# Memory of the first two cross batches split in the dense phase, their keys and values projected ahead of the turn of the queries

## What is computed

```python
attn_out = jnp.where(vm, ctx @ v_dense, ctx @ l_dense)
hidden_states = residual + attn_out
ci = rms_norm(hidden_states, ln_post_cross_w)
cq = heads(ci @ cq_w, NH, CHD)                 # cross queries, 16 heads of 16
ckv = encoder_outputs @ ckv_w                  # encoder_outputs is the memory
ck, cv = jnp.split(ckv, 2, axis=-1)
cctx = sdpa(heads(cq), heads(ck), heads(cv), causal=False)
hidden_states = hidden_states + cctx @ cdense_w
```

## Time and profile before

| | us |
|---|---|
| median of three runs | 2365.92 |
| the profiled execution: span from its first to its last instruction | 2358.2 |
| median less span | 7.7 |
| TensorE busy | 2198.0 (93%) |
| VectorE busy | 1336.0 (57%) |
| ScalarE busy | 1072.2 (45%) |
| GpSimd busy | 880.1 (37%) |
| mean granted TensorE clock | 0.984 of full speed |

### The profile page before, as it was taken

How to read it: one execution, slowest core, us unless ns; L and a number is a source line. 1 busy time by engine, 2 the same in 40 slices (tenths; PEclk the granted TensorE clock), 3 DMA queues, 4 the chain that set the end, 5 groups by cost and what they waited for, 6 DMA issues and landing times.

```text
span 2358.2 us, 46947 instructions
## 1 busy us (share of the span) xinstructions
PE 2198.0 (93%) x19542; PEld 1834.5 (78%) x19542; DVE 1336.0 (57%) x1919; ACT 1072.2 (45%) x1842; POOL 880.1 (37%) x738
## 2 busy tenths in 40 slices
PE   6899998999989989987999999998899999999998
PEld 5799986887766668876777777776788888888887
DVE  5655545877779994436666666663534444435332
ACT  4344434343167774533555555553543334334332
POOL 1201117677524324531122111110655455455553
PEclk9999999999989999998999999999999999999999
DMA  6434325565364436642111111111644333443331
GB/s 199 139 118 140 126 87 184 189 244 207 132 205 136 140 110 238 253 147 67 41 40 50 41 44 47 39 35 47 222 132 155 120 130 120 145 132 115 110 112 45
DMA packets 107058, 293.58 MB, mean 124 GB/s; under 512 B 14424, under 2 KB 18360, under 8 KB 100216
## 3 DMA queue, kind: packets, MB, share of 16 engines
q1 hardware_dynamic: 86624, 229.63, 30.1%
q0 software_dynamic: 18720, 60.29, 7.0%
q10 hardware_dynamic: 1504, 0.68, 0.1%
HBM read 221.36 MB, written 69.18 MB: 123 GB/s over the span
## 4 chain that ended last, share of the span: by engine, by line
PE 78%; DVE 9%; ACT 7%; DMA 3%; issue 2%; POOL 1%; SPq 0%; POOLq 0%; DVEq 0%; ACTq 0%
PE ps L109 19%; PE ps L111 18%; PE ps L110 18%; PE ps L1593 4%; PE ps L1612 3%; PE ps L1630 3%; DVE f_arena L979 3%; ACT f_arena L1508 2%; PE ps L1146 2%; ACT f_arena L1094 1%; DMA f_arena<-mem_n 1%; PE ps L620 1%; DVE f_arena L975 1%; PE ps L1157 1%; DVE f_arena L971 1%
## 5 line engine op out<-in xcount | busy, mean ns | idle before, releaser
L109 PE MATMUL ps<-r_arena 128*128 128x512 f32 (+6 forms) x2410 | 902.3, 374 | 44.7 <-DVE r_arena L177 19.8
L177 POOL TENSOR_TENSOR r_arena<-f_arena,r_arena 128x512 fp32r<-128x512 f32 (+1 forms) x438 | 587.8, 1366 | 872.0 <-ACT r_arena L1489 437.2
L111 PE MATMUL ps<-r_arena 128*128 128x512 f32 (+6 forms) x2410 | 881.5, 366 | 0.0
L110 PE MATMUL ps<-r_arena 128*128 128x512 f32 (+6 forms) x2410 | 880.9, 366 | 0.0
L109 PEld LDWEIGHTS ps<-r_arena 128*128 128x128 f32 (+2 forms) x2410 | 454.2, 188 | 137.5 <-issue 32.4
L111 PEld LDWEIGHTS ps<-r_arena 128*128 128x128 f32 (+2 forms) x2410 | 454.0, 188 | 65.3
L110 PEld LDWEIGHTS ps<-r_arena 128*128 128x128 f32 (+2 forms) x2410 | 454.8, 189 | 59.8
L199 ACT CAST r_arena<-f_arena 128x512 fp32r<-128x512 f32 x400 | 235.5, 620 | 168.9 <-PE ps L111 135.8
L1726 DVE TENSOR_REDUCE e_negmax<-ps 112x3 f32<-112x1125 f32 (+1 forms) x160 | 225.2, 1408 | 104.9 <-PE ps L1593 102.2
L1508 ACT ACTIVATE f_arena<-ps 125x1792 f32<-125x1792 f32 x96 | 159.9, 1666 | 98.2 <-PE ps L1615 97.9
L2011 DVE SCALAR_TENSOR_TENSOR f_arena<-f_arena,ps 128x512 f32<-128x512 f32 (+1 forms) x88 | 57.4, 652 | 233.9 <-ACT f_arena L1901 233.9
(11 more groups left out here) (201 smaller groups left out, 2733.8 us busy)
## 6 DMA issues: line engine op xcount, KB each, us to landing
f_arena<-weights SPq DMA_DIRECT2D x400, 256.0 KB, 3.0
f_arena<-rows SPq DMA_DIRECT2D x14, 1160.0 KB, 5.2
f_arena<-qk_rows SPq DMA_DIRECT2D x32, 448.0 KB, 3.9
f_arena<-mem_e SPq DMA_DIRECT2D x32, 376.0 KB, 3.2
f_arena<-mem_t SPq DMA_DIRECT2D x16, 750.0 KB, 9.6
f_arena<-mem_n SPq DMA_DIRECT2D x8, 1500.0 KB
h_rows<-f_arena SPq DMA_DIRECT2D x7, 1160.0 KB, 4.3
f_arena<-h_rows SPq DMA_DIRECT2D x7, 1160.0 KB, 5.2
```

The costliest lines, as they stand in the source:

```text
L109: first = pe.matmul(out, w_hi, x_hi, start=start, stop=False)
L110: pe.matmul(out, w_hi, x_lo, start=False, stop=False)
L111: return first, pe.matmul(out, w_lo, x_hi, start=False, stop=stop)
L177: return engine.tensor_tensor(out, source, high.bitcast(F32), ALU.subtract)
```

## The change

- SyncE issues the memory loads of batches 0 and 1 at the start of the dense phase, behind the first loads of context and rows (`d_sp`), and no longer in front of the wait for the scatters.
- ScalarE makes the high parts of these two memories in the dense phase, in its turns n = 1 and 2, behind the ring's casts and ahead of the squares; GpSimd makes the low parts in its turns n = 2 and 3, behind the ring's low parts and ahead of the power.
- TensorE makes the key products of batch 0 in the last turn of the dense phase, between `turn_normed(7)` and `queries(7)`, and into banks 0 and 1 (`e_key_bank`), which need only the last additions of the dense result to be done. `keys` is split in two: `e_key_products` and `queries_turn`.
- At the start of the cross phase TensorE makes values(0) into banks 2 and 3, waits for `d_cq_out`, makes the key products and values of batch 1 (banks 4 to 7), and only then turns the queries of batch 0 and makes its first scores. In step 0 only `queries_turn(1)` is left of the keys and values of batch 1.
- ScalarE and VectorE copy both batches' values out before they split keys and queries of batch 0. VectorE no longer waits for the values before it writes the ones.
- `scores(0, 0)` now waits for the copies of batch 0's values, since these lie in banks 2 and 3 that the scores write.

The diff, cut to its core:

```diff
+        def e_memory_high(act, b):
+            act.wait_ge(e_m_loaded[b % 2], 16 * (b // 2 + 1))
+            if b >= 2:
+                act.wait_ge(e_v, 2 * (b - 1))
+            act.copy(e_m_parts[b % 2][0], e_m[b % 2]).then_inc(e_m_hi, 1)
+        def e_memory_low(pool, b):
+            pool.wait_ge(e_m_hi, b + 1)
+            low(pool, e_m_parts[b % 2][1], e_m[b % 2], e_m_parts[b % 2][0]).then_inc(e_m_lo, 1)
+        def e_key_bank(b):
+            return 4 if b else 0
+        def e_key_products(pe, b):
+            pe.wait_ge(e_m_lo, b + 1)
+            if b >= 3:
+                pe.wait_ge(e_exp, KEY_UNITS * (b - 2))
+            hi, lo = e_m_parts[b % 2]
+            for t in range(CT):
+                for k in range(CT):
+                    w = slice((t * CT + k) * P, (t * CT + k + 1) * P)
+                    split_products(pe, ps[:, e_key_bank(b) + t, 0:CEVEN], e_w_hi[:, 0, w], e_w_lo[:, 0, w],
+                                   hi[:, k, :], lo[:, k, :], k == 0, k == CT - 1)
 def d_sp(sp):
...
             load_rows(1)
+            for b in range(2):
+                sp.dma_start(e_m[b], mem_e[b]).then_inc(e_m_loaded[b], 16)
             for n in range(TILES):
 def d_pool(pool):
...
                         ring_low(pool, m)
+                if 2 <= n < 4:
+                    e_memory_low(pool, n - 2)
                 if n < TILES:
                     pool.wait_ge(*d_mean.at(n + 1))
 def d_act(act):
...
                         ring_high(act, m)
+                if 1 <= n < 3:
+                    e_memory_high(act, n - 1)
                 if n < TILES:
 def d_pe(pe):
...
                     dense(n, 3)
+                if n == TILES:
+                    pe.wait_ge(d_h, BLOCKS)
+                    e_key_products(pe, 0)
                 if n:
                     queries(n - 1)
 def e_sp(sp):
...
-            load_memory(0)
-            load_memory(1)
             sp.wait_ge(*d_scattered.at(16 * BLOCKS))
 def e_pool(pool):
...
-            memory_low(0)
-            memory_low(1)
 def e_act(act):
...
-            memory_high(0)
-            memory_high(1)
+            values(0)
+            values(1)
             keys_queries_high(0)
-            values(0)
 def e_pe(pe):
...
             def scores(b, u):
                 if u == 0:
                     pe.wait_ge(e_kq_lo, 3 * (b + 1))
+                    if b == 0:
+                        pe.wait_ge(e_v_act, 1)
+                        pe.wait_ge(e_v_dve, 1)
...
-            pe.wait_ge(d_h, BLOCKS)
+            values(0, range(NKC))
             pe.wait_ge(d_cq_out, BLOCKS // 2)
-            keys(0)
-            values(0, range(NKC))
+            e_key_products(pe, 1)
+            values(1, range(NKC))
+            queries_turn(0)
             scores(0, 0)
             for s in range(BATCHES):
-                if s < 2:
-                    pe.wait_ge(e_v_act, s + 1)
-                    pe.wait_ge(e_v_dve, s + 1)
+                if s == 1:
+                    pe.wait_ge(e_v_act, 2)
+                    pe.wait_ge(e_v_dve, 2)
+                if 2 <= s + 1 < BATCHES:
+                    e_key_products(pe, s + 1)
                 if s + 1 < BATCHES:
-                    keys(s + 1)
+                    queries_turn(s + 1)
...
 def e_dve(dve):
...
-            dve.wait_ge(e_v, 2)
             for i in range(3):
                 dve.memset(e_cv[i][:, :, :, CHD:2 * CHD], 1.0).then_inc(e_ones, 1)
             dve.memset(ones_r.bitcast(F32), 1.0).then_inc(e_ones, 1)
+            values(0)
+            values(1)
             keys_queries_low(0)
-            values(0)
             maximum(0, 0)
```

More of the change, by code:

```diff
@@ L1237, in build_xattn @@
         d_x_parts = both(16384, (KT, TILE))
+        e_m_loaded, e_cq_loaded = ([sem(f"e_{n}_loaded{i}") for i in range(2)] for n in ("m", "cq"))
+        e_m_hi, e_m_lo, e_k, e_v, e_kq_hi, e_kq_lo, e_v_act, e_v_dve = (sem(n) for n in (
+            "e_m_hi", "e_m_lo", "e_k", "e_v", "e_kq_hi", "e_kq_lo", "e_v_act", "e_v_dve"))
+        e_exp = sem("e_exp")
+        e_m = [fv(16000 + 752 * i, (CT, CEVEN)) for i in range(2)]
+        e_m_parts = [both(22528 + 1504 * i, (CT, CEVEN)) for i in range(2)]
+        def e_memory_high(act, b):
[18 more added lines that the diff above has]
+                                   hi[:, k, :], lo[:, k, :], k == 0, k == CT - 1)
         def d_sp(sp):
@@ L1414, in d_dve @@
                     dve.tensor_scalar(t_ss[:, n % 2, 0:tb(n)], t_ss[:, n % 2, 0:tb(n)], EPS, None, ALU.add).then_inc(d_mean.sem, 1)
-        e_m_loaded, e_cq_loaded = ([sem(f"e_{n}_loaded{i}") for i in range(2)] for n in ("m", "cq"))
-        e_m_hi, e_m_lo, e_k, e_v, e_kq_hi, e_kq_lo, e_v_act, e_v_dve = (sem(n) for n in (
-            "e_m_hi", "e_m_lo", "e_k", "e_v", "e_kq_hi", "e_kq_lo", "e_v_act", "e_v_dve"))
-        e_s, e_maxed, e_mx, e_mxt, e_mxt_made, e_st, e_exp, e_ctx, e_raw, e_turned, e_normed, e_back = (sem(n) for n in (
-            "e_s", "e_maxed", "e_mx", "e_mxt", "e_mxt_made", "e_st", "e_exp", "e_ctx", "e_raw", "e_turned", "e_normed",
-            "e_back"))
+        e_s, e_maxed, e_mx, e_mxt, e_mxt_made, e_st, e_ctx, e_raw, e_turned, e_normed, e_back = (sem(n) for n in (
+            "e_s", "e_maxed", "e_mx", "e_mxt", "e_mxt_made", "e_st", "e_ctx", "e_raw", "e_turned", "e_normed", "e_back"))
         e_c_hi, e_c_lo, e_cd, e_cd_out, e_ones = (sem(n) for n in ("e_c_hi", "e_c_lo", "e_cd", "e_cd_out", "e_ones"))
         e_scattered = [Later(done, 8 * BATCHES) for done in c_scattered]
-        e_m = [fv(16000 + 752 * i, (CT, CEVEN)) for i in range(2)]
         e_cq = [fv(17504 + 256 * i, (CDIM,), SEQ) for i in range(2)]
@@ L1431, in build_xattn @@
         e_out = [fv(18016 + 512 * i, (DIM,), SEQ) for i in range(2)]
-        e_m_parts = [both(22528 + 1504 * i, (CT, CEVEN)) for i in range(2)]
         e_k_parts = [both(8192 + 1504 * i, (CT, CEVEN)) for i in range(3)]
@@ L1464, in e_pool @@
         def e_pool(pool):
-            def memory_low(b):
-                pool.wait_ge(e_m_hi, b + 1)
-                low(pool, e_m_parts[b % 2][1], e_m[b % 2], e_m_parts[b % 2][0]).then_inc(e_m_lo, 1)
             def store(b):
@@ L1500, in values @@
                 act.wait_ge(e_v, 2 * b + 1)
-                act.copy(e_cv[b % 3][:, 0:2, :, 0:CHD], ps[0:KC, 6, :].rearrange("p (c h d) -> p c h d", c=2, h=HEADS)).then_inc(
+                act.copy(e_cv[b % 3][:, 0:2, :, 0:CHD], ps[0:KC, e_key_bank(b) + 2, :].rearrange("p (c h d) -> p c h d", c=2, h=HEADS)).then_inc(
                     e_v_act, 1)
@@ L1551, in e_pe, with queries_turn @@
         def e_pe(pe):
-            def keys(b):
-                pe.wait_ge(e_m_lo, b + 1)
-                if b >= 3:
-                    pe.wait_ge(e_exp, KEY_UNITS * (b - 2))
-                hi, lo = e_m_parts[b % 2]
-                for t in range(CT):
-                    for k in range(CT):
-                        w = slice((t * CT + k) * P, (t * CT + k + 1) * P)
-                        _, last = split_products(pe, ps[:, 4 + t, 0:CEVEN], e_w_hi[:, 0, w], e_w_lo[:, 0, w],
-                                                 hi[:, k, :], lo[:, k, :], k == 0, k == CT - 1)
+            def queries_turn(b):
                 pe.wait_ge(e_cq_loaded[b % 2], 16 * (b // 2 + 1))
                 for t in range(CT):
-                    last = pe.transpose(ps[:, 4 + t, CEVEN:CEVEN + SEQ], e_cq[b % 2][:, t * P:(t + 1) * P],
+                    last = pe.transpose(ps[:, e_key_bank(b) + t, CEVEN:CEVEN + SEQ], e_cq[b % 2][:, t * P:(t + 1) * P],
                                         ident[0:SEQ, 0:SEQ])
@@ L1573, in values @@
                     m = slice(c * KC, (c + 1) * KC)
-                    out = ps[0:KC, 6 + c // 2, (c % 2) * CDIM:(c % 2 + 1) * CDIM]
+                    out = ps[0:KC, e_key_bank(b) + 2 + c // 2, (c % 2) * CDIM:(c % 2 + 1) * CDIM]
                     for k in range(CT):
@@ L1743, in keys_queries_low @@
             def keys_queries_low(b):
+                at = e_key_bank(b)
                 dve.wait_ge(e_kq_hi, 3 * (b + 1))
-                low(dve, e_k_parts[b % 3][1], ps[:, 4:6, 0:CEVEN], e_k_parts[b % 3][0]).then_inc(e_kq_lo, 1)
+                low(dve, e_k_parts[b % 3][1], ps[:, at:at + CT, 0:CEVEN], e_k_parts[b % 3][0]).then_inc(e_kq_lo, 1)
                 hi, lo = (x.rearrange("p (t x) s -> p t x s", t=CT) for x in e_q_parts[b % 3])
                 for x in range(2):
-                    dve.scalar_tensor_tensor(lo[:, :, x, :], ps[:, 4:6, CEVEN:CEVEN + SEQ], cmask[:, x:x + 1],
+                    dve.scalar_tensor_tensor(lo[:, :, x, :], ps[:, at:at + CT, CEVEN:CEVEN + SEQ], cmask[:, x:x + 1],
                                              hi[:, :, x, :].bitcast(F32), ALU.mult, ALU.subtract).then_inc(e_kq_lo, 1)
```

27 lines of the change are left out of this document (11 added, 16 removed).

## The result

The changed kernel took 2356.62 us (median of 5 runs, 2355.88 to 2359.85) against 2366.54 us of the kernel before (5 runs, 2364.51 to 2368.18): a ratio of 0.9957, 95% interval 0.9947 to 0.9968. Two later comparisons, each with the kernel before on the same chip, gave 0.9971 (0.9958 to 0.9984) and 0.9969 (0.9958 to 0.9980). The medians differ by 9.9, 7.1 and 6.3 us; the forecast was 7.46. The profiled execution of after spans 2354.7 us, only 3.5 us less than that of before.

What follows compares the result with a forecast made beforehand. Bound: the seam between dense and cross phase, where TensorE waits. Batch 0's scores at 1059.81 plus 14.15 gives batch 1's at 1073.96, 7.46 us earlier; 2365.92 - 7.46 = 2358.5 us, range 2355.8 to 2363.2.

Steps and rivals of the forecast that it cites:

- the ring: Dense phase: GpSimd's power step, scatters, SyncE's wait, next tile's loads, which ScalarE and GpSimd await; makes up little delay.
- The fill of the 2.47 us wait: End of dense phase: batch 0's 12 key products, 2.04 us, fit TensorE's wait for VectorE's last split, 0.4 us spare.
- The first scores: Start of cross phase: batch 0's scores start at 1059.81, 6.19 us earlier, after load, turn, ScalarE's copies and VectorE's split.
- Batch 1's first scores: Cross phase: batch 1's scores start at 1073.96 in place of 1081.42, 7.46 us earlier at the low clock.
- The steps of 2.71, 5.52, 2.71 and 3.21 us: From batch 0's first scores to batch 1's: alternation of scores and VectorE's maximum at the low clock, 14.15 us together.
- What comes after: Beyond batch 1's first scores: nothing TensorE needs moves later; the clock returns after the same 5.7 us.
- part is handed back: Rival: dense delay of 3.56 us uncovered (gain 3.9), or clock returns 3 us later in batch 1's step (5.5); chance 0.16.
- the shift in the fourth batch: Cross phase: the prediction is wrong if the 7.5 us shift found at 1074 is gone in the fourth batch.
- The dense phase: Dense tiles: early memory loads, ScalarE's copies and GpSimd's passes cost nothing, with margins of 0.4 and 0.1 us.
- sign (6): Dense tiles at the same times as before, TensorE without a new gap near 905 and 967; gaps mean wrong.
- The full 3.56 us: Dense phase: both GpSimd passes, 1.78 us each, counted in full as delay of tile 3's power step.
- the 7.7 us between span and median: Whole kernel: profiled span 2358.2 against median 2365.92; the difference lies around the span and was left as is.

Runs made afterwards that it cites:

- keys0_late: The changed kernel with batch 0's key products moved behind the last cross queries, out of TensorE's earlier wait; ratio 0.9969 to the kernel before.
- busy: The changed kernel with dummy matmuls, whose results nothing reads, in TensorE's waits; ratio 0.9951 to the kernel before.
- memset_only: The kernel before with one line less: VectorE does not wait for the values before it writes the ones; ratio 0.9977 to the kernel before.
- busy_again: The changed kernel with dummy matmuls in TensorE's waits, the same kernel measured a second time; ratio 0.9927 to the kernel before, 2356.7 us.
- memset_busy: The kernel before with the memsets' wait removed and 50 dummy matmuls in TensorE's waits; ratio 0.9960 to the kernel before.

## Why the prediction was right, and where it was not

- **The fill of the 2.47 us wait**: right. 12 products took what was said, 0.19 us of the matmuls' wait (0.50 of the weight load's, forecast 0.4) are left, and the undo (`keys0_late`) gave 1.5 us back at the first scores. The bound of 2.04 us was its price with nothing else changed; at batch 3 it is 1.2 us.
- **The first scores**: predicted 1059.81, or 9.94 us after the landmark. Measured 1061.57 - 1051.23 = 10.34 in the first trace, 10.43 and 10.45 in the other two. (The second trace's maximum is 0.43 us earlier than the first's because its first scores still ran at the high clock, 0.77 us.) The terms stood (turn and hand-over 0.45, ScalarE 1.47, split with hand-over 1.7); what was short is the load's landing: issue 1.42 us later than before's 1054.38 at a landmark 1.36 us later, and 2.1 in place of 1.9 us.
- **Batch 1's first scores**: predicted 7.46 us earlier. The maxima give 7.06, 7.48 and 6.94 us. The steps of 2.71, 5.52, 2.71 and 3.21 us are in the trace after as 2.71, 5.52, 2.71 and 3.20, the low clock all through as forecast. The Trainium skill's rule to keep TensorE warm (TensorE: Matmul & The Clock Gate, "HAM oscillation — how this bites in real kernels") spoke against this change, and the trace agrees: 0.50 over 17 us, and `busy` shows what it cost, 2.2 us at batch 1 and 6.5 at batch 3.
- **What comes after**: here the argument failed in part. The rival "part is handed back" had the outcome but not the way: it let the clock return 3 us late in batch 1's step. I let the clock return 5.7 us after batch 1's first scores and took the rest as a shift. It returned sooner, after 4.4 us (near 1080.1), but then fell again from 1090 to 1097, for twice as long as before in the same step (from 1097 to 1101). In the first two traces 0.7 and 0.9 us of the gain went there by batch 3. In the third the clock was down for 3 us only, from 1092 to 1095, and nothing went (6.94 and 6.96). Of the signs that I named for a wrong prediction, the shift in the fourth batch (batch 3) is therefore met in part: 6.4 to 7.0 us of the 7.5 are there.
- **The dense phase**: right in the trace after, at no cost: from TensorE's turn of tile 0 to the landmark it is 157.67 us in both. In `busy` it is 158.42, with the wait of 0.43 us near 906 that sign (6) asked for: this margin is gone in two of nine traces. In the trace after the context of tile 2 took 10.9 us from 894.93 to land, at 905.83, and TensorE turned it at 906.78, straight behind its matmul: that is 905.42 plus the 1.36 us by which this trace runs late, and 0.95 us of margin where I had counted 0.4. The full 3.56 us that I carried to tile 3 were 2.6 to 3.3, and TensorE waited in none of these traces; doubling the passes confirmed the ring and, with 3.6 us as the delay that it covers, the 0.1 us that I counted behind the full 3.56.
- **Span and time**: the 7.7 us between span and median do not lie around the span, as I took it; 1.8 to 1.9 do, and the profiled execution was a short one. The forecast of the time did not suffer, since I worked from the median. The 2356.62 of the first comparison is 1.9 us under the forecast although the seam gave less than forecast (6.1 us at batch 31, not 7.46): nothing in the seam accounts for that, so it counts as luck.
- **The worth of the parts**: the sum did not ask what each part brings alone, and this is where the runs surprised. Without the memsets the dense-phase part is worth nothing or less; the memset line alone matches the whole. The forecast total was right, but a reader who takes from it that the early memory loads earn the gain would be wrong.

## What to carry to other kernels

A wait that the chain of waits puts down to one engine is not that engine's worth: ask what is late next when it goes (here a load that hung on the scatters, 3.73 us behind), and try each edit alone, since one line bought what the whole change did. Where several engines alternate in short steps, moving TensorE's work out of them leaves it at its low clock; with dummy matmuls in its waits the same order gained another 4.4 to 6.5 us by batch 3. Compare traces by distances from a landmark close to the edit, not by spans, and look also at what lies ahead of the landmark.

## What the runs showed of the hardware

Executions of one kernel on one chip spread over 11 us (2359.12 to 2370.27). The two traces of before differ by 7.3 us, of which 3.9 arise up to the end of the cross phase and 3.1 behind it, with a granted clock of 1.00 in one and 0.90 in the other from 1600 to 1650, while before's seam repeats within 0.04 us. And a thin stretch costs beyond its end: the order of the work in the steps of batches 1 and 2 is the same in all these kernels, yet the way from batch 1's first maximum to batch 3's took between 31.6 us (`busy`) and 36.1 us (`keys0_late`). It follows the time that the clock was low in it, from the granted clock over each of these stretches: 31.6 us with none, 32.7 with 2.2 us low (`memset_only`), 33.1 with 3.4 (`busy_again`), 34.6 with 6.8 (`memset_busy`), 35.1 with 7.8 (before), 35.8 with 9.9 (after) and 36.1 with 10.3 (`keys0_late`). So a microsecond at the low clock cost some 0.4 us of time there, TensorE being at work for most of it. This is also how the one line keeps up with the whole change: it arrives at batch 1 2.1 to 2.6 us later, but has 2.2 and 2.4 us of low clock on the way to batch 3 where the changed kernel has 7.7 to 10.2. Why the clock falls again in batch 2's step in the one and not in the other is not shown.
